# Two GNN layers on one core: four groups' rows are gathered from x in stage one, and the row ring grows from four to eight

## The reference

```
x = layernorm(x + GAT(x, edges))          # layer 0: 4 heads of 32
    xl = x @ W_l; xr = x @ W_r            # GAT, with a self loop for each node
    e  = sum_c(att * leaky_relu(xl[src] + xr[dst], 0.2))
    p  = softmax of e over the edges of one dst
    out = layernorm(sum(p * xl[src]) + bias + x) * gamma + beta
x = layernorm(x + MLP(2x + sum over edges of (x[src] + edge_attr)))   # layer 1
```

## Time and profile before

| what | us |
|---|---|
| median of three runs | 4075.12 |
| profiled execution | 4078.24 |
| its span | 4076.4 |
| stage one | 0 to about 76 |
| layer 0 | 76 to about 2075 |
| layer 1 | from about 2098 |

### The profile page before, as it was taken

One profiled execution on the slowest core, in us unless ns is written; L12 is line 12 of the kernel. 1 busy time (PEld: TensorE's weight loads), 2 busy tenths in 40 slices (PEclk: granted clock), 3 DMA queues, 4 the chain that ended last, 5 costly groups with the idle time before them and its releaser, 6 DMA issues. The chain is left out here.

```text
span 4076.4 us, 80602 instructions
## 1 busy us (share of the span) xinstructions
PE 3042.1 (75%) x19237; PEld 2546.8 (62%) x19238; DVE 2101.4 (52%) x8183; ACT 1598.5 (39%) x3438; POOL 2993.8 (73%) x3200
## 2 busy tenths in 40 slices
PE   7888888888888888888846666666666666666666
PEld 6666666666666666666636666565666665666665
DVE  6777777777777777777743222222222222322222
ACT  5555555555565655555612212112121212121111
POOL 3777777777777777777737777777777777777776
PEclk9999999999999999999978888888888888888888
DMA  7545455554555454545444444444444444444443
GB/s 232 141 130 137 133 136 133 135 133 133 135 134 137 132 135 130 135 130 136 131 89 124 117 118 117 117 117 122 118 117 117 117 118 119 121 117 118 117 117 92
DMA packets 446506, 518.24 MB, mean 127 GB/s; under 512 B 198373, under 2 KB 346536, under 8 KB 446472
## 3 DMA queue, kind: packets, MB, share of 16 engines
q1 hardware_dynamic: 266390, 268.21, 21.7%
q0 software_dynamic: 100032, 208.27, 21.5%
q10 hardware_dynamic: 80050, 41.37, 3.6%
HBM read 470.23 MB, written 47.29 MB: 127 GB/s over the span
## 5 line engine op out<-in xcount | busy, mean ns | idle before, releaser
L1588 POOL DMA_INDIRECT rows<-x_table,src_idx x1563 | 1487.3, 952 | 530.0 <-issue 530.0
L762 POOL DMA_INDIRECT rows<-xl_table,src_idx x1563 | 1489.6, 953 | 479.0 <-issue 456.7
L846 PE MATMUL pA<-wmsg,edge_of 128*128 128x136 f32 x3126 | 405.6, 283 | 123.7 <-DVE edge_of L1247 123.1
L989 ACT ACTIVATE relu_h<-ph 128x512 f32<-128x512 f32 x391 | 231.3, 597 | 616.0 <-PE ph L804 616.0
L1611 PE MATMUL pA<-edge_of,dst_row 128*128 128x128 f32 x1568 | 304.0, 373 | 226.1 <-DMA rows<-x_table,src_idx 215.9
L846 PEld LDWEIGHTS pA<-wmsg,edge_of 128*128 128x128 f32 x3126 | 379.1, 190 | 134.5 <-issue 131.6
L1718 ACT ACTIVATE relu_h<-ph,b 128x128 f32<-128x128 f32 x196 | 72.0, 367 | 976.3 <-PE ph L1668 864.0
L1611 PEld LDWEIGHTS pA<-edge_of,dst_row 128*128 128x128 f32 x1568 | 283.4, 279 | 241.6 <-issue 240.9
L1611 PE MATMUL pT<-node_of,dst_row 128*128 128x128 f32 x1558 | 294.4, 367 | 181.2 <-DMA rows<-x_table,src_idx 172.1
L804 PE MATMUL ph<-node_of,xr_win 128*128 128x512 f32 (+1 forms) x782 | 411.8, 652 | 7.0 <-issue 6.6
L1044 ACT ACTIVATE node_of<-dst_row,first_node 128x1024 f32<-128x1024 int32 x196 | 405.5, 2069 | 2.4 <-DVE first_node L1158 2.4
(11 more groups left out here) (207 smaller groups left out, 5454.4 us busy)
## 6 DMA issues: line engine op xcount, KB each, us to landing
dst_row<-in_dst SPq DMA_DIRECT2D x195, 513.0 KB
dst_row<-in_edge_attr SPq DMA_DIRECT2D x195, 512.0 KB
rows<-xl_table,src_idx POOLq DMA_INDIRECT x1563
rows<-x_table,src_idx POOLq DMA_INDIRECT x1563
sums_table<-win ACTq DMA_DIRECT2D x196, 68.0 KB
xr_win<-xr_table SPq DMA_DIRECT2D x196, 64.0 KB
relu_h<-x_table SPq DMA_DIRECT2D x196, 64.0 KB
out_x<-relu_h ACTq DMA_DIRECT2D x193, 64.0 KB
```

What stands on the lines that cost most here:

```text
L762: pool.indirect_dma_start(rows[s][:, t, 0:DW], None, xl_table[:, :], bass.IndirectOffsetOnAxis(ap=src_idx[s][:, t:t + 1], axis=0))\
L846: ins = pe.matmul(pA[k][:, 0:WC], edge_of[k][:, t, :], w[:, t, :], start=(t == 0), stop=(t == tiles(g) - 1))
L989: act.activation(relu_h[0][:, k:to, :], ph[0][:, k:to, :], ACT.Relu, scale=1.0 - GAT_SLOPE)\
L1588: pool.indirect_dma_start(rows[s][:, t, 0:D], None, x1_table[:, :], bass.IndirectOffsetOnAxis(ap=src_idx[s][:, t:t + 1], axis=0))\
```

## The change

In stage one GpSimd no longer adds the linear part of the self loops. It waits for the edge numbers of groups 0 to 3 and gathers the rows of **x** that they name, 32 gathers of 128 rows, into a part of the tile `sums` that is free until the merges (`pre_rows`). The linear part is added in each merge instead, by one more linked step of VectorE. At layer 0's head, ahead of group 0, TensorE turns those rows into table rows, in 16 pairs of tiles: two transposes (`turn_pre`), VectorE's copy, two products with the 132 columns of W_l and the linear part (`multiply_pre`), and VectorE's copy back into `pre_rows` (`convert`). The 24 matmuls without a reader go.

From then on there are eight row buffers, the four of `rows` and the four of `pre_rows`, and eight buffers of edge numbers. Group g uses row buffer (g + 4) modulo 8; GpSimd starts layer 0 with group 4. Since buffers are chosen when the program is written, the bodies of layer 0's loops on all engines now hold eight steps, with 23 rounds and a tail of twelve steps.

```diff
-AHEAD = 3
+RING = 2 * U
+            step(Group(j, c, RING), lambda g: (regs[2 * (g.c - lo)], regs[2 * (g.c - lo) + 1]))
+
+    loops = (groups - back - (RING - 1)) // RING
+    done = RING * loops
+    part(None, 0, range(back), 0, max(2, back))
+    with eng.Fori(0, loops) as j:
+        part(j, 0, range(back, RING + back), 0, RING + max(2, back))
+    part(None, done, range(done + back, groups + back), done, groups - done)
+        pre_rows = sums[:, :, :].rearrange("p b k -> p (b k)")[:, 0:U * T * PITCH].rearrange("p (s t k) -> p s t k", s=U, t=T)
+        rows_of_slot = [t[:, :, :] for t in rows] + [pre_rows[:, s] for s in range(U)]
+        pre_pairs = [(g, t) for g in range(U) for t in range(0, T, 2)]
+        pre_x = [relu_h[1][:, t:t + 2, :] for t in range(0, T, 2)]
+
+        def row_slot(g):
+
+            return (g.c + U) % RING
-                def add_linear(q):
-                    pool.wait_ge(S("self_summed"), q.times(1, 1))
-                    e_of = e_self_pair[:, q.times(1)]
-                    pool.tensor_tensor(e_of, e_of, ring_w[q.c % R][:, :, D:DW], ALU.add).then_inc(S("e_made"), 1)
-
-                node_loop(pool, pairs, [(add_linear, 0)])
+                for k in range(U):
+                    pool.wait_ge(S(f"src_in0{k}"), 16)
+                    for t in range(T):
+                        pool.indirect_dma_start(pre_rows[:, k, t, 0:D], None, a["x"][:, :],
+                                                bass.IndirectOffsetOnAxis(ap=src_idx[k][:, t:t + 1], axis=0))\
+                            .then_inc(S(f"gathered0{U + k}"), 16)
+            linear = msets[:, k0:k1, at_xl:at_xl + 2 * DW].rearrange("p f (b d) -> p f b d", b=2)[:, :, :, D:DW]
             link(v.tensor_scalar(by_node(tmp), den, 0.0, -BIG, ALU.is_le, ALU.mult))
+            link(v.tensor_tensor(by_node(self_), by_node(self_), linear, ALU.add))
+                for k in range(U):
+                    sp.wait_ge(S(f"gathered0{U + k}"), 16 * T)
 
+                def gather(g):
+                    k, s = g.c % RING, row_slot(g)
+                    wait_alone(pool, pool_waits, S(f"src_in0{k}"), g.use(16, 16, RING))
+                    wait_alone(pool, pool_waits, S(f"rows_free0{s}"), (g + U).use(1, 0, RING))
+                    for t in range(tiles(g)):
+                        pool.indirect_dma_start(rows_of_slot[s][:, t, 0:DW], None, xl_table[:, :],
+                                                bass.IndirectOffsetOnAxis(ap=src_idx[k][:, t:t + 1], axis=0))\
                             .then_inc(S(f"gathered0{s}"), 16)
+                with pool.Fori(0, (groups - U) // RING - 1) as j:
+                    for c in range(U, U + RING):
+                        gather(Group(j, c, RING))
+                for c in range(groups - RING, groups):
+                    gather(Group(None, c, RING))
-                for _ in range(24):
-                    pe.matmul(pA[0][:, 0:P], ident[:, :], ident[:, :], start=True, stop=True)
+                def turn_pre(k):
+                    g, t = pre_pairs[k]
+                    if t == 0:
+                        pe.wait_ge(S(f"gathered0{U + g}"), 16 * T)
+                    if k >= 2:
+                        pe.wait_ge(S("xT_ready"), pairs + k - 1)
+                    for b in range(2):
+                        ins = pe.transpose((pT1, pT2)[k % 2][:, b * P:(b + 1) * P], pre_rows[:, g, t + b, 0:D], ident[:, :])
+                    ins.then_inc(S("x_taken"), 1)
+
+                def multiply_pre(k):
+                    pe.wait_ge(S("xT_ready"), pairs + k + 1)
+                    if k >= 2:
+                        pe.wait_ge(S("xl_ready"), pairs + k - 1)
+                    for b in range(2):
+                        ins = pe.matmul(lr_bank[k % 2][:, b, 0:DW], pre_x[k % len(pre_x)][:, b, :], w_lr[:, 0:DW],
+                                        start=True, stop=True)
+                    ins.then_inc(S("lr_ready"), 1)
+
+                for k in range(len(pre_pairs) + 1):
+                    if k < len(pre_pairs):
+                        turn_pre(k)
+                    if k >= 1:
+                        multiply_pre(k - 1)
+                pe.wait_ge(S("xl_ready"), pairs + len(pre_pairs))
+                        pe.wait_ge(S("near_row_made"), 1)
-                v.tensor_copy(near_row, node_row[:, :]).then_inc(S("near_row_made"), 1)
-                v.wait_ge(S("near_row_made"), 1)
+
+                def convert(first, last):
+                    for k in range(first, last):
+                        if k < len(pre_pairs):
+                            v.wait_ge(S("x_taken"), pairs + k + 1)
+                            v.tensor_copy(pre_x[k % len(pre_x)], (pT1, pT2)[k % 2][:, 0:2 * P].rearrange("p (b n) -> p b n", b=2))\
+                             .then_inc(S("xT_ready"), 1)
+                        if k >= 1:
+                            g, t = pre_pairs[k - 1]
+                            v.wait_ge(S("lr_ready"), pairs + k)
+                            v.tensor_copy(pre_rows[:, g, t:t + 2, 0:DW], lr_bank[(k - 1) % 2][:, :, 0:DW]).then_inc(S("xl_ready"), 1)
+
                 link = Chain(v, S("head_chain")).link
 
...
```

VectorE's step 0 calls `convert` in three parts, between its other preparations; `near_row` is made after them, and TensorE waits for it ahead of `attend` of group 0:

```diff
+                        half = len(pre_pairs) // 2
+                        convert(0, half + 1)
                         prepare(g)
                         first_of(g)
+                        convert(half + 1, half + 5)
                         homes_of_merges()
                         first_of(g + 1)
+                        convert(half + 5, 2 * half + 1)
                         starts_of_steps()
+                        v.tensor_copy(near_row, node_row[:, :]).then_inc(S("near_row_made"), 1)
+                        v.wait_ge(S("near_row_made"), 1)
```

More of the change, by code:

```diff
@@ L91, in sweep, with part @@
 def sweep(eng, groups, step, ends=None, layer=0, back=1):
[L95 removed]
+    pool = []
+    def part(j, first, steps, lo, n):
         regs = []
         if ends is not None:
[L98 to L99 removed]
+            while len(pool) < 2 * n:
+                pool.append(eng.alloc_register(f"ends{layer}_{len(pool)}"))
+            regs = pool[0:2 * n]
+            eng.load(regs, ends[0:1, bass.ds(2 * first if j is None else j * (2 * RING), 2 * n)])
         for c in steps:
[L101 to L107 removed]
+            step(Group(j, c, RING), lambda g: (regs[2 * (g.c - lo)], regs[2 * (g.c - lo) + 1]))
[5 more added lines that the diff above has]
+    part(None, done, range(done + back, groups + back), done, groups - done)
 def walk(eng, tag, groups, step, back, extra=0, wants=(), unrolled=0):
@@ L177, in build @@
     pairs = blocks // 2
[L178 removed]
+    assert groups % U == 0 and groups > 2 * RING and (groups - U) % RING == 0 and pairs % UP == 0 and pairs > UP
     assert nodes - 2 * UP * P <= real <= nodes - SPAN
@@ L575, in merge_of @@
         def merge_of(g):
-            return Group(g.j, (g.c - 1) // U, 1)
+            return Group(g.j, (g.c - 1) // U, RING // U)
         act_last = []
```

75 lines of the change are left out of this document (27 added, 48 removed).

## The result

The changed kernel takes 4139.54 us (median of four runs, 4134.58 to 4141.39), the kernel before beside it 4074.45 us: a ratio of 1.0157, with an interval of 1.014 to 1.0175. It is slower by 65 us, where 20 were forecast and the range ended at 4116. The way and the mechanism were as forecast, the size was not. The profiled execution took 4138.8 us (span 4137.0), beside 4078.24 of before.

What follows compares the result with a forecast made beforehand. GpSimd's gathers bound layer 0; afterwards its consumers would: group 195 at 134.4 + 1893 - 24 + 6 + 2 = 2011, plus 62 for missed pages, 2073, 20 us later than before. Forecast 4095 us, range 4034 to 4116.

Steps and rivals of the forecast that it cites:

- GpSimd and stage one: Stage one: 32 gathers of x, 40.2 us, hidden in GpSimd's idleness; stage one 2 us longer (bounds 0 and 6).
- Layer 0's head: Ahead of group 0: 16 pairs take 18.4 us; group 0's sources at 99, group 4 at 134.4 in place of 132.19.
- The store of four pages: VectorE's instruction store keeps four pages; the 603-instruction loop misses its first page at each of 22 returns, 62 us.
- The rival that the store keeps the longer loop: Layer 0's loops: no page is read again, the gathers' limit rules, 4037 us; chance 0.21.
- The price of a missed page: VectorE's return in layer 0: 2.8 us each, taken between DRAM reads of 2.5 and 3.7 us; 62 us in all.
- The end of the loop itself: Layer 0's loop ends: 48 x 1.22 = 59 us becomes 22 x 1.6 = 35 without the page, 24 less.
- the merges' longer chain and stage one: One more linked VectorE step in 49 merges adds 6 us to the consumers' time, stage one 2.
- The pace between the ends: The consumers in layer 0 take 9.91 us a group, loop ends included: 1893 us for 191 groups.
- the term for the return: Each of 22 returns of layer 0's loop: 1.6 us for the end and 2.8 for VectorE's missed page.
- its upper end: The dear price of VectorE's missed page, 3.7 us a return: group 195 at 2092, 4115 us.
- The forecast's first rival: The instruction store keeps the longer loop, so GpSimd's gathers rule layer 0: 4037 us; chance 0.21.
- The limit of the gathers: GpSimd's gathers in layer 0 let group 195 start at 2014.8, 38 us ahead of 2053.01.

Runs made afterwards that it cites:

- e14: e13 with VectorE's loop as in the changed kernel (603 instructions, checks for second windows included): 4135.77 us, ratio 1.0147 to the kernel before.
- e17: The kernel of e3 run on another chip, against the kernel before: 4232.02 us, ratio 1.0381.
- e18: The changed kernel with the eight transposes of the sources issued three times more on TensorE at each return: 4133.63 us, ratio 1.0133 to the kernel before.
- e2: The kernel before with a never-entered block in VectorE's four-step loop (363 instructions, still three pages): 5958.9 us on a disturbed chip, kernel before 5941.7.
- e3: The kernel before with two never-entered blocks in VectorE's four-step loop (446 instructions, four pages): 5980.6 us on a disturbed chip, kernel before 5941.7.
- e7: The changed kernel with VectorE's loop cut to 370 instructions on three pages, second-window code and checks left out: 4134.51 us, ratio 1.0144 to the kernel before.
- e13: e7 with ScalarE's loop shortened too and SyncE's dst-number loads held until the load of sums lands: 4038.45 us, ratio 0.9906 to the kernel before.
- e16: e13 with two blocks of 65 never-entered instructions in VectorE's loop: 4055.63 us, ratio 0.995 to the kernel before.

## Why the prediction was wrong in size

- **GpSimd and stage one**: right. The gathers of x are hidden, and the first of layer 0's stands at 80.16, 2.7 us behind 77.49, where 2 were taken.
- **Layer 0's head**: group 0 at 97.74 for 99. But group 4 at 137.14 for 134.4: the 4.7 us that groups 1 and 2 no longer wait for gathers were not all on the path. Groups 0 to 4 take 39.4 us, 0.75 less than before, and not 4.7 less. An error of 2.7 us.
- **The store of four pages**: right, in kind and number (100 and more packets forecast, 270 found), and VectorE's loop is what loses by it (e14, e17). The loop covers six pages by its packets, not five; that changes nothing here. The rival that the store keeps the longer loop fell with the first row read.
- **The price of a missed page**: mis-sized. 2.8 us was taken between rows of 2.5 and 3.7; VectorE's branch measures 3.65 us in place of 0.27, so 3.4. Over 22 returns that is 13 us too little.
- **The end of the loop itself**: mis-sized. The whole end was put at 4.4 us, of which 1.6 without the page, from TensorE's 1.22 at 634.99. The engine that mattered was VectorE, whose own end costs 1.6 us before (11.75 for 10.17 in the table) and, with a table of twenty entries, 0.5 more. With the page this is 5.8 us measured for 4.4, 31 us over the returns, the page's 13 among them.
- **Missing from the sum**: the step behind the return, 1.0 us slower than in the tail (up to 0.7 of it the fallen clock, by e18), 23 us; the round's second half, 0.9 slower (0.66 of it two jumps onto another page), 21 us; and leaving the loop, 3 us. Against these stand 8 us that had been set aside for the merges' longer chain and stage one.
- **The pace between the ends**: mis-sized the other way. The forecast had (1893 - 59) / 191 = 9.60 us a group; the tail goes at 9.42, which is 35 us less over 191 groups. The 9.91 was measured over returns that cost VectorE 1.6 us and 0.7 in the step behind, and only 1.22 was taken off for each.

Together, from group 4 to group 195: 31 + 23 + 21 + 3 - 8 - 35 = 35 us, of the 38 that the stretch took longer than forecast; with the head's 2.7 these are the 40 us between 2073 and 2113. What failed is the term for the return: 22 x 4.4 us, of which 2.8 for the page, where the runs show 22 x 5.8 and 1.0 more in each step behind. Its mechanism stood; its price was worked out from TensorE's idle time and two DMA rows while VectorE carried it, and its upper end (3.7 us for the page, 4115) allowed for nothing but the page.

That "slower" came out right is in part luck. With the tail's pace and all else as it was, the forecast's own sum would have given 2073 - 35 = 2038 for group 195, ahead of the 2053.01 of before. Two errors, a pace too slow and ends too cheap, stood against each other.

The Trainium skill, Runtime: NRT & Kernel Launch (Instruction fetch mechanics), gives most engines 32 KiB of instruction memory and TensorE 128 KiB, and has a taken branch wait for its page when that is not held. The runs agree: 32 KiB are four pages of 8192 bytes, and e2, e3 and e7 have the bound between three pages with one ahead and four with one ahead. TensorE's longer loop stayed inside (three packets on q8 in 1880 us). The same section calls the cost of going on into a next block mostly hidden; the rows agree (pages are read all through a round, and its third and fourth steps take 9.26 and 8.56 us, as in the tail).

The forecast's first rival is worth a look back: with the page kept, the checks gone and the sums' load in time the kernel takes 4038 us (e13), for the 4037 worked out for it. The limit of the gathers was worked out rightly, and 37 us can be had when the consumers keep up. That the changed kernel would reach it with its page kept and its checks in place is an estimate (79.7 us a round for 80.4), not shown.

## What to carry to other kernels

Count a hardware loop's instructions for each engine before lengthening its body, and look at the packets of the "instruction" queue in one round: none, and the loop is kept; otherwise the loop covered one page fewer than there were packets. On VectorE and ScalarE a body on three pages of 128 instructions returned in 0.20 to 0.27 us and one on four or more in 2.4 to 3.7 us (medians). Code that is never entered counts like any other (e3, e17). Price a stop on the engine that carries the path through that step, from that engine's own steps with and without it, and take a pace between ends from a stretch that has none. What a stop costs depends on what else is waited for: one missed page a round cost 155 us in e17 and 17 in e16. And when an engine gets faster, look at which transfers change their order: in e7 a load that slipped behind 513 KB took back the whole gain.

## What was not expected of the hardware

- A return to a missed page takes 3.4 us more than one to a kept page on VectorE in the changed kernel, 3.0 more in e16 and e17, and 2.7 more on ScalarE in the changed kernel (2.9 for 0.20); a jump of some 14 instructions onto another page 0.48 us in place of 0.15, and one over 65 instructions 0.98 us.
- TensorE fell to half its clock (granted 0.53, targets at 3.69 us for 1.88) behind 3.46 us of waiting and 1.92 us at its own loop's end; with 24 more transposes in that time the targets ran at 1.00 again.
- The load of sums (136 KB) took 2.4 us from issue to the landing of its last part when it was issued 0.2 us ahead of another queue's 513 KB, and 5.8 when it was issued 0.1 us behind them (the merges near 1160 us in the changed kernel and e7).
